# P times V with V stationary, four heads side by side in column tiles

## The chip, the cores and the metric

The kernel runs on one core of one Trainium2 chip. The metric is the device time of one execution, in microseconds (us). Three executions of the kernel before took 3895.41 us in the median, 3886.71 to 3902.54.

## What is computed

Four layers run one after the other over 16 sequences of 256 tokens and 256 channels: layer 0 (two state-space scans, one forward and one backward in time), layer 1 (one scan, with a gather of the tokens by an index and back), layer 2 (attention with 16 heads of 16 channels) and layer 3 (attention with softmax over queries' channels and over keys' tokens). The change touches layer 2 alone. Its core:

```python
q = (xn @ q_w + q_b).reshape(Bx, Tx, H, -1)          # H = 16, 16 channels each
k = (xn @ k_w + k_b).reshape(Bx, Tx, H, -1)
att = jnp.einsum('bnhl,bmhl->bnmh', q, k)
att = att + (1.0 - mask) * -1000000.0
att = jax.nn.softmax(att, axis=2)
v = ((xn @ v_w + v_b) * src_mask[:, :, None]).reshape(Bx, Tx, H, -1)
y = jnp.einsum('bnmh,bmhl->bnhl', att, v).reshape(Bx, Tx, Dx)
```

All numbers are fp32. "P" below is the exponential of the scores, not yet divided by its sum; V carries a 17th column of ones per head, so that the product also holds that sum.

## The kernel before

**Scan units.** The scans are cut into 1,536 units, 96 per batch: three scans (two of layer 0, one of layer 1) of 16 states in two halves of the channels. A unit is a chain over all engines: ACT (line 638) and POOL (line 647) scale the input into `dbut`, PE transposes it into PSUM (`ps_b`, line 563), DVE scans along time (line 667) with the decays that ACT makes (line 628), POOL multiplies the states by C (line 682), which SP has loaded from DRAM six units ahead (line 702, two units in a load), and PE transposes and sums the results in `ps_y` (line 591). The buffers are few (three of `dbut`, `hst` and `g`, four of `decay`), and all engines are in order.

**Ticks and side pieces.** Time in the program is counted in ticks, one per unit. Everything else, the *side pieces*, is written as generators per layer, stage and engine, which stop at each `yield next(at)`. The table `PLACES` gives the tick of every piece, counted from the base of its period; a period is 96 ticks (`PERIOD`). `Between` runs all pieces that are due at a tick: on DVE behind the tick's scan, on SP behind its load of C, on PE between the transposes of unit t+2 (line 563) and the sum of unit t-2 (line 591). In period i the stages belong to different batches: the scans of layer 0 to batch i, layer 1 to i-1 and i-2, the first part of layer 2 (`l2a`) to i-2, its second part (`l2b`), its end (`l2_tail`) and layer 3 to i-3. So the instruction stream is fixed when it is built, and a piece that comes too early holds up its engine.

**The end.** The last scans (32 units of layer 1) start 64 ticks into period 16. `l2b` at ticks 2 to 42 thus runs beside scans for batches 0 to 12, ahead of the last scans for batch 13, and behind all scans for 14 and 15.

**Layer 2.** `l2a` makes `qT` and `kT` (channels of a head on 32 partitions, of which 16 are used and one or two carry the mask and the row maximum; the 16 heads fill four blocks of 128 partitions) and `v2`, computes the scores once for their maxima (line 1263) and transposes the maxima back. `l2b` goes in eight groups of two heads: PE makes the transposed scores of both heads into two PSUM banks (line 1289, `ps_x` banks 0 and 1, keys on partitions, four matmuls of 18 rows by 256), ACT takes their exponential into `pT` (line 1339, 128x1024), and PE multiplies with V (line 1303) into bank 2, P^T stationary in blocks of 128x128, 17 columns of V moving, for 2 heads x 2 blocks of queries x 2 blocks of keys. `pT` exists once, so the exp of a group waits for the product of the last (semaphore `o_full_2`), and the next scores wait for the exp (`p_ready`). The scores of group g stand in the stream ahead of the product of group g-1. After eight heads DVE takes reciprocals of the sums and multiplies (lines 1379 and 1382) into `yv`, and signals `o_taken_2`, for which PE waits before the next eight heads.

`l2_tail` then normalizes, modulates and projects `yv`; `xt_x` is the buffer that it and `l2a` use for turned input. The DMAs that the prediction speaks of are side pieces on SP: the mask of layer 3 (line 1405, which waits for `res_1`, the sum that DVE makes at line 1177), the store of the result (line 1411, which waits for `res_3`) and the loads for layer 0 (lines 889 and 890).

## Time and profile before

| | |
|---|---|
| median of three executions | 3895.41 us (3886.71 to 3902.54) |
| the profiled execution's own time | 3887.06 us |
| its span | 3885.3 us |
| mean granted clock of TensorE | 0.938 of full speed |
| first scan to last scan | 152.5 to 3644.2 us |
| instructions in the span | 66,431 |

One execution was profiled. Its page gives busy times by engine; PE is TensorE's matmuls, PEld its weight loads, which overlap them, DVE is VectorE, ACT ScalarE, POOL GpSimd, SPq the DMA queue of SyncE. A fp32 matmul that is no transpose leaves two records of each kind, a transpose one. The waits give, for each engine that sat idle, what released it. The span is a little shorter than the execution's own time, which is the one that is compared.

### The profile page before, as it was taken

Reading aid. Unit: us, or ns where it says so; the run is one execution under the profiler, and the core shown is the slowest. Engines: PE = TensorE matmul, PEld = TensorE weight load, DVE = VectorE, ACT = ScalarE, POOL = GpSimd, SP = SyncE. Lnnn points to the kernel's source line nnn. Section 1 sums busy time; section 2 is a strip of 40 time slices with the busy share of each in tenths; the row PEclk is TensorE's granted clock in tenths of the full one; section 3 lists DMA queues with packets and bytes.
Section 4 is the critical chain, followed back from the end, with each engine's and each line's share of the span. In section 5 each row is a group of like instructions: output and inputs, shape, how many; then the busy total and the mean of one; then the engine's idle time right before and its main releaser. Section 6 shows DMA issues by size and latency. Waiting matters only on the chain. (4 is left out here: it accounts for less than half of the span.)

```text
span 3885.3 us, 66431 instructions
## 1 busy us (share of the span) xinstructions
PE 3405.1 (88%) x22974; PEld 2923.2 (75%) x22974; DVE 2839.1 (73%) x3589; ACT 2898.8 (75%) x6592; POOL 2859.1 (74%) x3087
## 2 busy tenths in 40 slices
PE   4677788999999998999999998999999899898876
PEld 2466677888888787888878787878878787876655
DVE  0468788787887878787887878787878878773421
ACT  1668788788888888888888788888888788854422
POOL 0478999888887888788888888887888878861400
PEclk9799999999999999999999999999999999997766
DMA  4112222222122212222221212222222212210100
GB/s 163 49 54 80 79 71 79 66 65 78 59 85 59 80 61 79 63 66 78 60 83 59 82 61 80 62 73 69 66 78 61 83 58 73 63 54 18 39 7 3
DMA packets 140814, 257.19 MB, mean 66 GB/s; under 512 B 15905, under 2 KB 33313, under 8 KB 140081
## 3 DMA queue, kind: packets, MB, share of 16 engines
q1 hardware_dynamic: 140482, 252.95, 21.2%
q8 instruction: 186, 3.05, 0.3%
q14 instruction: 146, 1.20, 0.1%
HBM read 233.16 MB, written 5.05 MB: 61 GB/s over the span
## 5 line engine op out<-in xcount | busy, mean ns | idle before, releaser
L682 POOL TENSOR_TENSOR g<-hst,c_bc 128x512 f32<-128x512 f32 x1536 | 1978.3, 1288 | 569.4 <-PE ps_y L591 415.9
L667 DVE TENSOR_TENSOR_SCAN hst<-decay,ps_b 128x512 f32<-128x512 f32 x1536 | 1835.6, 1211 | 509.6 <-PE ps_b L563 244.4
L628 ACT ACTIVATE decay<-delta,acoef 128x256 f32<-128x256 f32 x3072 | 1376.9, 498 | 11.4 <-DVE hst L667 11.0
L563 PE MATMUL ps_b<-ident,dbut 128*128 128x128 f32 x6144 | 964.7, 281 | 267.0 <-DVE hst L667 151.8
L647 POOL TENSOR_TENSOR dbut<-dut,bcm 128x256 f32<-128x256 f32 x1536 | 982.8, 640 | 217.9 <-ACT dut L853 217.9
L563 PEld LDWEIGHTS ps_b<-ident,dbut 128*128 128x128 f32 x6144 | 724.9, 145 | 347.0 <-issue 234.7
L591 PE MATMUL ps_y<-ident,g 128*128 128x128 f32 x6144 | 959.6, 280 | 14.7 <-issue 7.3
L591 PEld LDWEIGHTS ps_y<-ident,g 128*128 128x128 f32 x6144 | 760.5, 145 | 119.3 <-issue 35.2
L638 ACT ACTIVATE dbut<-dut,bcm 128x256 f32<-128x256 f32 x1536 | 767.1, 500 | 53.7 <-PE ps_b L563 50.3
L1303 PEld LDWEIGHTS ps_x<-v,pT 128*128 128x128 f32 x2048 | 276.6, 213 | 31.9 <-issue 28.0
L1303 PE MATMUL ps_x<-v,pT 128*128 128x17 f32 x2048 | 282.6, 277 | 3.2 <-ACT pT L1339 2.3
L1339 ACT ACTIVATE pT<-ps_x 128x1024 f32<-128x1024 f32 x128 | 129.4, 1011 | 123.4 <-PE ps_x L1303 116.1
L1289 PE MATMUL ps_x<-qT,kT 18*128 18x256 f32 x1024 | 164.8, 444 | 20.5 <-ACT pT L1339 19.6
L1364 DVE TENSOR_REDUCE mxt<-ps_x 128x4 f32<-128x1024 f32 x128 | 153.4, 1199 | 12.5 <-PE ps_x L1263 12.5
L1263 PE MATMUL ps_x<-kT,qT 17*128 17x256 f32 x1024 | 149.9, 411 | 6.5 <-DVE mxt L1364 4.2
L617 ACT ACTIVATE xm<-ps_y 128x512 f32<-128x512 f32 x64 | 38.2, 597 | 134.9 <-PE ps_y L591 134.8
L1289 PEld LDWEIGHTS ps_x<-qT,kT 18*128 18x128 f32 x1024 | 98.3, 207 | 54.0 <-ACT pT L1339 27.4
L760 PE MATMUL ps_v<-weights,yg 128*128 128x256 f32 x512 | 133.1, 396 | 3.3 <-DVE yg L1169 1.7
L754 PE MATMUL ps_v<-xt_a,weights 128*128 128x256 f32 x512 | 134.3, 392 | 0.2
L754 PE MATMUL ps_x<-xt_x,weights 128*128 128x256 f32 x512 | 128.2, 390 | 5.2 <-ACT xt_x L1315 5.2
L1263 PEld LDWEIGHTS ps_x<-kT,qT 17*128 17x128 f32 x1024 | 90.3, 190 | 38.8 <-issue 20.4
L860 DVE SCALAR_TENSOR_TENSOR delta<-ps_v,delta 128x512 f32<-128x512 f32 x96 | 64.8, 675 | 62.0 <-ACT delta L841 61.9
(188 smaller groups left out, 4092.1 us busy)
## 6 DMA issues: line engine op xcount, KB each, us to landing
c_bc<-c_rows SPq DMA_DIRECT2D x768, 256.0 KB, 3.2
rows_bc<-mod_rows SPq DMA_DIRECT2D x16, 384.0 KB, 4.4
weights<-in_weights_dram SPq DMA_DIRECT2D x1, 5792.0 KB
ada_w<-in_ada_w_dram SPq DMA_DIRECT2D x1, 5120.0 KB
x<-in_x_dram SPq DMA_DIRECT2D x16, 256.0 KB, 3.8
x0p<-x SPq DMA_DIRECT2D x16, 256.0 KB, 2.5
xr<-x SPq DMA_DIRECT2D x16, 256.0 KB, 3.6
x<-x SPq DMA_DIRECT2D x16, 256.0 KB, 3.6
```

The lines of the kernel that those rows point to most:

```text
L563: last = nc.tensor.matmul(ps_b[:, u % 2, e * T + t * P:e * T + (t + 1) * P], dbut[:, u % NDBU, t, e * P:(e + 1) * P], ident[:, :], is_tran ...
L591: last = nc.tensor.matmul(ps_y[:, t, e * P:(e + 1) * P], g[:, u % NG, e, t * P:(t + 1) * P], ident[:, :], is_transpose=True, start=False, ...
L628: last = nc.scalar.activation(decay[:, u % (DA_AHEAD + 2), e, :], delta[s][:, eb, :], ACT.Exp, scale=acoef[:, s, eb, n:n + 1])
L638: nc.scalar.activation(dbut[:, u % NDBU, 0, :], dut[s][:, 0, hh * HALF * P:(hh + 1) * HALF * P], ACT.Copy, scale=bcm[s][:, 0, n:n + 1]).th ...
L647: nc.gpsimd.tensor_tensor(dbut[:, u % NDBU, 1, :], dut[s][:, 1, hh * HALF * P:(hh + 1) * HALF * P], bcm[s][:, 1, n:n + 1].broadcast_to([P, ...
L667: nc.vector.tensor_tensor_scan(line(hst[:, u % NHST, :, :].rearrange("p e t -> p (e t)")), line(decay[:, u % (DA_AHEAD + 2), :, :].rearran ...
L682: nc.gpsimd.tensor_tensor(g[:, u % NG, :, :], hst[:, u % NHST, :, :], c_bc[:, k % NCB * CHUNK + n % CHUNK, :].unsqueeze(1) .broadcast_to([ ...
L754: last = nc.tensor.matmul(dst, weight[:, k, m0:m0 + m], rhs[:, k, :], start=(k == 0), stop=(k == kb - 1))
L1263: last = nc.tensor.matmul(bank(ps_x, j, TB)[:, q, :], qT[r:r + DH2 + 1, hb, q * P:(q + 1) * P], kT[r:r + DH2 + 1, hb, :], start=True, stop ...
L1289: last = nc.tensor.matmul(bank(ps_x, j, TB)[:, m, :], kT[r:r + DH2 + 2, hb, m * P:(m + 1) * P], qT[r:r + DH2 + 2, hb, :], start=True, stop ...
L1303: last = nc.tensor.matmul(o[:, q, :], pT[:, j, m, q * P:(q + 1) * P], v2[:, m, v, :], start=(m == 0 and q == 0 and v % 8 == 0), stop=(m == ...
L1364: nc.vector.tensor_reduce(by_head[:, 2 * g_:2 * g_ + 2, :, DH2 + 1], ps_x[:, 0:2, :].rearrange("p j (q n) -> p j q n", q=TB), AX.X, ALU.ma ...
```

## The change

- **Groups.** A group of `l2b` is no longer two heads with all keys, but four heads with one block of 128 keys (`half, k, m = g_ // 4, g_ // 2 % 2, g_ % 2`). The scores are still four matmuls of 18 rows by 256, and the exp is still one instruction of 128x1024.
- **The product.** V's 17 columns are stationary, 256 queries of P^T move; four matmuls per group write to partitions 0, 32, 64 and 96 of one half of bank 2, the second block of keys accumulates on the first. The output has a head's channels on partitions.
- **Turned back.** After four groups ACT copies bank 2 to `oT` (the buffer `xt_x`), 128x512, and PE turns it by four transposes into bank 2, in the layout that DVE expects. New semaphores: `ot_sb` and `o_back`. DVE waits for `o_back` instead of `o_full_2`.
- **Heads permuted.** `spread` puts heads in other slots of the query, key and bias layouts, so that the four heads of a group stand in the row tiles that the scores need.
- **Prologue.** One memset of bank 2, since 15 of 32 partitions are never written.
- **Places.** New ticks for side pieces on all engines, most by 0 to 2 ticks, those on SP by more. `l2b` has 19 pieces on PE instead of 25.

```diff
+        oT = xt_x
...
+                    done(nc.vector.memset(ps_x[:, 2, :], 0.0))
...
@@ l2b_tensor
-                    for m in range(TB):
-                        for j in range(2):
-                            h = 2 * g_ + j
-                            r, hb = LANE * (h % HPB), h // HPB
-                            last = nc.tensor.matmul(bank(ps_x, j, TB)[:, m, :], kT[r:r + DH2 + 2, hb, m * P:(m + 1) * P],
-                                                    qT[r:r + DH2 + 2, hb, :], start=True, stop=True)
+                    half, k, m = g_ // 4, g_ // 2 % 2, g_ % 2
+                    for j in range(4):
+                        r, hb = LANE * (2 * k + j % 2), 2 * half + j // 2
+                        last = nc.tensor.matmul(bank(ps_x, j % 2, 2)[:, j // 2, :], kT[r:r + DH2 + 2, hb, m * P:(m + 1) * P],
+                                                qT[r:r + DH2 + 2, hb, :], start=True, stop=True)
...
-                        for q in range(TB):
-                            for m in range(TB):
-                                last = nc.tensor.matmul(o[:, q, :], pT[:, j, m, q * P:(q + 1) * P], v2[:, m, v, :],
-                                                        start=(m == 0 and q == 0 and v % 8 == 0), stop=(m == TB - 1),
-                                                        skip_group_check=True)
+                    half, k, m = (g_ - 1) // 4, (g_ - 1) // 2 % 2, (g_ - 1) % 2
...
+                    for j in range(4):
+                        last = nc.tensor.matmul(bank(ps_x, 2, 2)[LANE * j:LANE * j + DH2 + 1, k, :],
+                                                v2[:, m, 8 * half + 4 * k + j, :], pT[:, j % 2, j // 2, :],
+                                                start=(m == 0 and k == 0), stop=(m == TB - 1), skip_group_check=True)
+                    last.then_inc(S["o_full_2"], 1)
+                if g_ in (H2 // 4, H2 // 2):
+                    yield next(at)
+                    pe.wait_ge(S["ot_sb"], nth("ot_sb", b, g_ // (H2 // 4)))
+                    for k in range(2):
+                        for q in range(TB):
+                            last = nc.tensor.matmul(bank(ps_x, 2, TB)[:, q, k * P:(k + 1) * P], oT[:, k, q * P:(q + 1) * P],
+                                                    ident[:, :], is_transpose=True, start=True, stop=True)
+                    last.then_inc(S["o_back"], 1)
@@ l2b_scalar
+                if g_ % 4 == 3:
+                    yield next(at)
+                    act.wait_ge(S["o_full_2"], nth("o_full_2", b, g_ + 1))
+                    nc.scalar.activation(oT[:, :, :], bank(ps_x, 2, 2), ACT.Copy).then_inc(S["ot_sb"], 1)
@@ l2b_vector
-                dve.wait_ge(S["o_full_2"], nth("o_full_2", b, (half + 1) * H2 // 4))
+                dve.wait_ge(S["o_back"], nth("o_back", b, half + 1))
@@ PLACES, three of the lines
     "l1_in": {
-        "DVE": (2, 7, 13, 14, 15, 15, 16, 19, 19, 20, 22),
+        "DVE": (-4, 7, 12, 14, 14, 15, 15, 18, 18, 19, 21),
     "l2b": {
-        "PE": (2, 4, 11, 12, 14, 14, 15, 19, 19, 21, 25, 26, 26, 29, 29, 29, 31, 32, 34, 36, 36, 38, 40, 40, 42),
+        "PE": (2, 4, 12, 14, 14, 18, 21, 25, 26, 27, 29, 29, 32, 34, 37, 37, 39, 40, 40),
     "l3": {
-        "SP": (9, 18, 95, 171),
+        "SP": (6, 6, 99, 211),
```

How the stream moves, at three places. First PE in a full period, the third group of `l2b` (tick 14) and what stands around it. Before (1289 scores, 1303 product, 591 and 563 the scans' sum and transposes, 754 a projection of layer 0):

```order
L1289 MATMUL ps_x<-qT,kT 128x256 x4
L1303 MATMUL ps_x<-v,pT 128x17 x4
L591 MATMUL ps_y<-ident,g 128x128 x4
L563 MATMUL ps_b<-ident,dbut 128x128 x4
L1303 MATMUL ps_x<-v,pT 128x17 x4
L754 MATMUL ps_v<-xt_b,z1w 128x256 x2
```

Now (1290 scores, 1300 product, 593 and 565 the scans', 756 the projection):

```order
L1290 MATMUL ps_x<-qT,kT 128x256 x4
L1300 MATMUL ps_x<-pT,v 17x256 x4
L756 MATMUL ps_v<-xt_b,z1w 128x256 x2
L593 MATMUL ps_y<-ident,g 128x128 x4
L565 MATMUL ps_b<-ident,dbut 128x128 x4
```

The product is one piece of four matmuls instead of two pieces of four. Second, PE at the end of the first eight heads (ticks 26 to 29), now; 1309 are the transposes back, 781 a projection for a scan:

```order
L1300 MATMUL ps_x<-pT,v 17x256 [waits p_ready]
L1300 MATMUL ps_x<-pT,v 17x256 x3
...
L1309 MATMUL ps_x<-ident,xt_x 128x128 [waits ot_sb]
L1309 MATMUL ps_x<-ident,xt_x 128x128 x3
...
L1290 MATMUL ps_x<-qT,kT 128x256 [waits p_ready]
L1290 MATMUL ps_x<-qT,kT 128x256 x3
L1300 MATMUL ps_x<-pT,v 17x256 [waits o_taken_2,p_ready]
L1300 MATMUL ps_x<-pT,v 17x256 x3
```

Between the product and the transposes stand one unit's sum and transposes, between these and the next scores two more units'. Before, the last product of the eight heads was followed by three units and the scores alone. Third, SP from the store of the result to the loads of C behind layer 3's mask. Before:

```order
L1411 DMA out_dram<-x 128x2x256
L702 DMA c_bc<-c_rows 128x512 x2
L1183 DMA gate<-mod_rows 128x256
L702 DMA c_bc<-c_rows 128x512 x3
L1226 DMA x<-x 128x512
L1405 DMA gate<-in_mask_dram 128x256
L702 DMA c_bc<-c_rows 128x512 x6
```

Now:

```order
L1420 DMA out_dram<-x 128x2x256
L704 DMA c_bc<-c_rows 128x512
L1228 DMA x<-x 128x512
L704 DMA c_bc<-c_rows 128x512
L1414 DMA gate<-in_mask_dram 128x256
L704 DMA c_bc<-c_rows 128x512 x13
```

The mask stands two loads behind the store instead of five, and the load of C behind it is the one placed at tick 8, for units 14 and 15.

## Rows read from the trace of the kernel before

**Rows 1.** The page, busy time (us), share of the span and instructions of the engines
```profile
span 3885.3 us, 66431 instructions
...
PE 3405.1 (88%) x22974; PEld 2923.2 (75%) x22974; DVE 2839.1 (73%) x3589; ACT 2898.8 (75%) x6592; POOL 2859.1 (74%) x3087
```

**Rows 2.** Periods: us, busy of PE, PEld, DVE, ACT, POOL; clock, DMA share, GB/s
```profile
295.30:488.50 193.20, 144.90 (x970) 124.11 (x970) 153.60 (x155) 157.01 (x370) 173.61 (x190) 0.94 0.25 76
488.50:682.80 194.30, 165.73 (x1144) 143.97 (x1145) 159.59 (x181) 159.81 (x378) 177.86 (x193) 0.96 0.24 74
682.80:898.00 215.20, 200.94 (x1429) 176.50 (x1428) 176.06 (x224) 179.75 (x411) 179.50 (x193) 0.98 0.22 69
2617.00:2833.00 216.00, 202.54 (x1418) 177.33 (x1418) 176.14 (x223) 176.78 (x404) 176.92 (x189) 0.96 0.23 67
```

**Rows 3.** Waits in the full periods, us in total, times, longest
```profile
POOL g L682 <- PE ps_y L591: 384.2, 402, 3.6
```

**Rows 4.** Chain of waits, uncovered layer 2: start us, us, engine, tile, line
```profile
3668.92 2.07 PE ps_x L1289 x8
3670.99 3.54 PE ps_x L1303 x16
3674.61 1.03 ACT pT L1339
...
3836.00 1.10 PE ps_x L747 x4
```

**Rows 5.** Timeline of PE in full periods: start us, us, line, op, out<-in, count
```profile
2648.50 0.96 PE L1303 MATMUL ps_x<-v,pT 128*128 128x17 f32 x8
2649.31 0.63 PE L747 MATMUL ps_v<-ident,xn_b 128*128 128x128 f32 x4
...
2652.38 1.03 PE L754 MATMUL ps_v<-xt_b,z1w 128*128 128x256 f32 x4
2653.24 0.60 PE L591 MATMUL ps_y<-ident,g 128*128 128x128 f32 x4
...
2766.54 0.60 PE L591 MATMUL ps_y<-ident,g 128*128 128x128 f32 x4
2766.98 0.60 PE L563 MATMUL ps_b<-ident,dbut 128*128 128x128 f32 x4
2767.51 1.13 PE L1263 MATMUL ps_x<-kT,qT 17*128 17x256 f32 x8
2768.57 0.66 PE L591 MATMUL ps_y<-ident,g 128*128 128x128 f32 x4
```

**Rows 6.** The page's groups: busy, mean ns of one, idle before, of P times V's loads
```profile
L1303 PEld LDWEIGHTS ps_x<-v,pT 128*128 128x128 f32 x2048 | 276.6, 213 | 31.9 <-issue 28.0
```

**Rows 7.** Groups of instructions: an ACT copy from PSUM of this size
```profile
L1114 ACT ACTIVATE xm<-ps_v 128x512 f32<-128x512 f32 x32 | 19.2, 599 | 80.5 <-PE ps_v L754 80.4
```

**Rows 8.** Uncovered windows, line 1303 alone: us, busy PE, PEld; clock, DMA share, GB/s
```profile
3469.50:3583.40 113.90, 23.01 (x128) 22.89 (x128) 0.73 0.06 19
3644.00:3886.00 242.00, 55.55 (x256) 53.91 (x256) 0.65 0.02 8
```

**Rows 9.** Timeline of DVE around the sum of layer 1
```profile
2647.95 0.69 DVE L1177 TENSOR_TENSOR x<-ps_v,xr 128x512 f32<-128x512 f32 x1
...
2650.86 1.22 DVE L667 TENSOR_TENSOR_SCAN hst<-decay,ps_b 128x512 f32<-128x512 f32 x1 [0.86 <-PE ps_b L563]
```

**Rows 10.** DMA issues: count, KB each, median us to landing
```profile
c_bc<-c_rows SPq DMA_DIRECT2D x768, 256.0 KB, 3.2
...
gate<-in_mask_dram SPq DMA_DIRECT2D x16, 128.0 KB, 2.9
```

**Rows 11.** Waits of the whole span, us in total, times, longest
```profile
DVE stats L717 <- DMA rows_bc<-mod_rows: 70.0, 15, 6.4
```

**Rows 12.** Timeline of DVE, the copy ahead of layer 1's norm
```profile
903.22 1.19 DVE L1045 COPY cols<-mod_cols 128x4 f32<-128x4 f32 x1
```

More of the change, by code:

```diff
@@ L160 @@
     "l3": {
-        "PE": (51, 52, 56, 58, 60, 63, 66, 68, 69, 70, 74),
-        "ACT": (49, 51, 61, 65, 66, 69, 70, 78),
-        "DVE": (49, 50, 58, 61, 63, 71, 71, 76, 76, 81, 97),
-        "SP": (9, 18, 95, 171),
+        "PE": (51, 52, 56, 58, 59, 62, 66, 68, 69, 70, 74),
+        "ACT": (50, 52, 60, 65, 66, 69, 70, 80),
+        "DVE": (50, 51, 58, 61, 63, 69, 71, 78, 80, 82, 102),
+        "SP": (6, 6, 99, 211),
     },
     "l3_tail": {
-        "PE": (83, 89, 91, 99),
+        "PE": (84, 90, 92, 103),
         "ACT": (87,),
@@ L1340, in l2b_scalar @@
                                      ps_x[:, 0:2, :].rearrange("p a n -> p (a n)"), ACT.Exp).then_inc(S["p_ready"], 1)
+                if g_ % 4 == 3:
+                    yield next(at)
+                    act.wait_ge(S["o_full_2"], nth("o_full_2", b, g_ + 1))
+                    nc.scalar.activation(oT[:, :, :], bank(ps_x, 2, 2), ACT.Copy).then_inc(S["ot_sb"], 1)
         def l2a_vector(dve, ch, b, at):
@@ L1654, in spread @@
         out = np.zeros((k, H2, 32), m.dtype)
-        out[:, :, :DH2] = m.reshape(k, H2, DH2)
+        slot = [h // 8 * 8 + h // 2 % 2 * 4 + h // 4 % 2 * 2 + h % 2 for h in range(H2)]
+        out[:, slot, :DH2] = m.reshape(k, H2, DH2)
         return out.reshape(k, H2 * 32)
```

76 lines of the change are left out of this document (35 added, 41 removed).

## The prediction

> **What bounds the kernel now.** I read the page's busy shares first [rows 1]: TensorE (PE) is busy 88% of the span, the others 73 to 75%. An average over stages can mislead, so next come the windows of single periods [rows 2]; a period is the 96 scan units of one batch, with its neighbours' side pieces between them. The first has no layer 2, the second the first part of one, the third everything, as all later ones (the fourth row). Going from second to third, PE's busy time rises by 35.2 us and the period by 20.9; DVE, ACT and POOL rise less, and PE ends at 201 of 215. The waits of the full periods [rows 3] say who is late: POOL, which multiplies the states by C, idles 384 us for PE's sums. So PE is the tightest engine there, though not the only one: POOL has 174 to 180 us of work in every period, and periods with less PE work still took 193 to 194 us.
>
> After the scans end, nothing covers layer 2. The chain of waits there [rows 4] is a strict round of scores (2.08), P times V (3.54) and exp (1.03), 6.8 us for each of eight groups; two batches run like that, and a third (3469.5 to 3583.4) nearly so, since the last scans start only after it.
>
> **What P times V costs now.** Per group 16 records of a fp32 matmul (each matmul leaves two), 128 columns of P^T stationary and 17 columns moving. In the timeline [rows 5] eight of them hold PE 0.81 us until the next instruction starts, so a group takes 1.62 and a batch 13.0 us. The page's row of their weight loads [rows 6] shows 277 us busy for 2048: a record is paced by loading 128 columns for 17 of work.
>
> **What it costs after.** A group is four matmuls, eight records: V (17 columns) stationary, 256 columns of P^T moving, each in its own column tile. No row shows column tiles. The nearest is the score product, which has 18 rows, so that neighbours lie in different row tiles. Full-array records of 256 columns take 0.86 us for four (line 754 in [rows 5]), 0.215 each, so eight would need 1.72. Eight records in two row tiles start the next instruction after 1.06 (line 1263 in [rows 5]): four steps of 0.215 and 0.20 of overhead. Entering that mode costs 0.10 more: it starts 0.53 after the previous four transposes began, where 0.44 is usual. So tiles do run side by side, two deep here, for 1.16 us a group.
> - Four column tiles at once, two steps: 1.16 - 0.43 = **0.73 us** a group. I take this, since the row tiles overlapped fully and nothing in the rows separates the two kinds.
> - Two at once: 1.16. One after another, the upper bound: 1.16 + 0.86 = 2.02. The lower bound is the 0.73, since a matmul's two records follow each other.
>
> The Trainium skill, "TensorE: Matmul & The Clock Gate", section "Measured speedup vs the span model", gives three column tiles 2.38 times one. As an estimate by that page, eight records would take 0.72 instead of 0.43 us, and the sum below would be about 23 us higher. No row here can check it.
>
> **The sum in the full periods.** Layer 2's second part runs under scans for 13 batches. Its eight groups cost 8 x 0.73 = 5.8, less 0.4 because in about half of them the product follows the scores directly and the mode change is already paid there. The new transposes back are 2 x 4 at 0.44 us per four (line 591 in [rows 5]): 0.9. Together 6.3 against 13.0: PE saves 6.7 us a batch, 87 in all. How much reaches the period? Rows 2 give 20.9/35.2 = 0.59 between the second and third, and that includes the flat part where POOL decides; at the top it can reach 1. I take 0.75: **-65 us**, ends -51 and -87.
>
> The two copies of PSUM to SBUF on ACT are 128x512 at 0.60 each [rows 7], 1.2 us a batch, beside 177 of 216 us of ACT work. Covered mostly; if ACT were the bound they would be 16 us in 13 batches. I take **+3**. The exp instructions stay eight per batch, and so do DVE's reciprocals and products, which now wait for the transposes instead of the product. PE reaches the next half's first product four groups of scan transposes and a score product after the turn back, so I cost its wait for DVE at nothing. If the wait for ACT's copy ahead of the turn back fails its place, PE stands still and the scans' transposes queue behind it, at most the copy and a little, 1 us a batch.
>
> **The sum without cover.** The product is busy 55.6 us in the last stretch and 23.0 in the one before the last scans [rows 8]. Cold (granted clock 0.65 in this window), the scores' eight records take 2.08 in four steps, so four column tiles take 2.08 - 2 x 0.43 = 1.22. Sixteen groups: 55.6 - 19.5 = 36. The other eight: 23.0 - 8 x 1.0 = 15, of which I count 10, because other pieces share PE there. Added: in each batch the first half's copy (0.60; its transposes lie beside the exp) and the second's copy, transposes (1.10, as line 747 in rows 4) and two hops, 1.9. 2.5 x 3 = 7.5. Net **-38**.
>
> **New places.** Most pieces move by 0 to 2 ticks; their order around the scans stays. Two moves are more.
> - On SP the mask load of layer 3 stands at tick 6 instead of 9, and its wait for the landing too, instead of at 18. It waits for the sum of layer 1, which DVE still makes at tick 12 (it ends at 2648.64 [rows 9]). Then 2.9 us of landing, and only then the load of C for unit 14, 3.2 us [rows 10]: about 2655.1 with both issues. The scan of unit 14 ends at 2652.1 [rows 9]. So POOL gets C 3 us late, and PE, which sums that unit two ticks later, 1.5 us. I take 1.5 x 13 = **+20**, ends 0 and 3 x 13 = 39. The store of the result stands on SP three ticks ahead of DVE's last addition (99 against 102), before it was two; C is loaded six units ahead, so I cost that at nothing.
> - DVE idles 70 us in 15 periods for the rows of layer 0, at tick -2 [rows 11]. The first norm of layer 1 moves from tick 2 to -4, ahead of this wait; its copy alone is 1.19 us [rows 12], with the statistics about 2. It fills idle time: -2 x 15 = -30 at most, 0 if POOL or ACT bind there; I take **-16**.
>
> The whole set can give or take 15 us more by the way stalls fall. The memset in the prologue is under 1 us.
>
> Sum: 3887 (the profiled execution; span 3885.3) - 65 + 3 - 38 + 20 - 16 = **3791 us**, 2.5% less. The profiled time equals the fastest of the three runs; their median is 8 us higher, which I leave within the range.
>
> **Rivals.**
> 1. *Slower: the column tiles do not overlap.* The instruction stream is A, A, B, B, and here all four tiles read the same 128 rows, while line 1263's tiles read different ones. If that is what allows overlap, a group costs 2.02 against 1.62. PE gains no 6.7 but loses 16.2 - 0.4 + 0.9 - 13.0 = 3.7 a batch, 48 x 0.75 = +36; without cover 16 x (3.80 - 3.54) = 4, about 3 for the third batch, and 7.5: +15. With the copies and places: **3945**. It decides from about six steps a group (0.30 + 6 x 0.215 = 1.59) on. Against it: row tiles overlap without loss. The Trainium skill states in the same page, section "The mechanism", that a weight load overlaps matmuls in flight only when the row group differs, which speaks for this rival. In the full-array stream the trace does not bear it out as a bar: records of one row group still follow each other every 0.215, loads hidden.
> 2. *Half overlap: two column tiles at a time.* 8 x 1.16 - 0.4 + 0.9 = 9.8 a batch, 3.2 less: x 13 x 0.75 = -31; without cover 16 x 1.46 + 6 - 7.5 = -22. With the rest: **3841.**
> 3. *The gain is covered.* PE gets shorter, but the periods stay, because POOL (174 to 180 us in each), scans and ACT's pieces set the pace, and places were made for other lengths. Only the uncovered stretches gain, with places and copies at +7: **3856**. For it: periods of 193 us with PE at 145. Against it: POOL's idle time ends on PE.
>
> **Chances.** Forecast 0.50 (own range 3745 to 3825: slope 0.59 to 1, places), rival 2 0.17, rival 3 0.13, rival 1 0.14, other losses by the new places near zero change 0.06. A measurement can tell about 0.5% (19 us) from no change. Faster by more: 0.50 + 0.17 + 0.09 of rival 3 = 0.76. Within: 0.04 of rival 3 and 0.04 = 0.08. Slower: 0.14 + 0.02 = 0.16. The range runs from 3740 to 3885; it leaves out rival 1 and little else.
>
> **What would show it.** Right: the product's records fall from 2048 to 1024, PE busy on them to 5 to 7 us a period, next instruction about 0.63 us after eight of them at full clock; full periods of 209 to 211 us; in the last stretch rounds of about 4.4 us instead of 6.8. Wrong: eight records that hold PE 1.9 us (rival 1) or 1.06 (rival 2), or records near 0.63 with periods still at 215 (rival 3), or a new idle time of PE in front of the transposes back, released by ACT.

## The result and the profile after

The changed kernel took 3852.34 us in the median (3834.64 to 3861.2), the kernel before 3887.25 (3873.91 to 3902.54) over the executions taken beside it: a ratio of 0.9898, 95% interval 0.9879 to 0.9917. It is 1.0% faster. The forecast was 3791 us, 2.5% less: the direction was right, the size was not.

The page of the changed kernel, its first lines as in [rows 1]:

```profile
span 3850.0 us, 64705 instructions
...
PE 3267.6 (85%) x22078; PEld 2693.0 (70%) x22078; DVE 2824.3 (73%) x3590; ACT 2918.2 (76%) x6624; POOL 2854.6 (74%) x3087
```

TensorE has 138 us less work than before, and the span is only 35 us shorter.

**The product itself did what was forecast, and a little more.** The timeline of PE in a full period of the changed kernel (start us, us, engine, line, op, out<-in, count), against [rows 5]. L1300 is the product:

```profile
2669.29 0.60 PE L565 MATMUL ps_b<-ident,dbut 128*128 128x128 f32 x4
2669.82 0.62 PE L1300 MATMUL ps_x<-pT,v 128*17 128x256 f32 x8
2670.38 0.66 PE L593 MATMUL ps_y<-ident,g 128*128 128x128 f32 x4
```

The next instruction starts 0.56 us after the first of the eight records. The group starts 0.53 after the transposes ahead of it, where 0.44 is usual, so it holds PE 0.65 in all, against 0.73 forecast and 1.62 before.

The chain of waits in the uncovered stretch of the changed kernel, two rounds and a way back (start us, us, what); it answers to [rows 4]:

```profile
3772.06 2.08 PE ps_x L1290 x8
3774.14 1.03 PE ps_x L1300 x8
...
3775.25 1.03 ACT pT L1344
...
3776.33 2.08 PE ps_x L1290 x8
3778.41 1.03 PE ps_x L1300 x8
...
3779.46 0.61 ACT xt_x L1349
...
3780.11 1.12 PE ps_x L1309 x4
```

A round takes 4.27 us (3772.06 to 3776.33), 6.8 before, 4.4 forecast. From the last scan to the end the kernel before needs 241.1 us, the changed one 203.5; the stretch ahead of the last scans, in which a third batch lies uncovered, fell from 113.9 to 95.4.

The load of the stationary columns does not stand in the way. The eight loads of the same group (PEld) take 0.13 us together, all four column tiles over the same 128 rows:

```profile
2669.82 0.13 PEld L1300 LDWEIGHTS ps_x<-pT,v 128*17 128x17 f32 x8 [0.17 <-issue]
```

**The full periods gained nothing.** These rows are the windows of the twelve full periods that begin with the third; divided by twelve, the busy times are per period. Layer 2's second part runs in these twelve and in the thirteenth, the "last part" below. First the kernel before, from 682.7 to 3263.8 (us; busy of PE, PEld, DVE, ACT, POOL; clock, DMA share, GB/s):

```profile
682.70:3263.80 2581.10, 2404.70 (x17106) 2109.53 (x17105) 2107.49 (x2673) 2154.66 (x4926) 2150.61 (x2302) 0.98 0.23 70
```

Then the changed kernel:

```profile
690.00:3290.10 2600.10, 2333.80 (x16436) 1967.23 (x16434) 2103.64 (x2673) 2172.43 (x4954) 2144.72 (x2302) 0.98 0.23 69
```

PE works 5.9 us less in a period (200.4 to 194.5), ACT 1.5 more (179.6 to 181.0), and a period went from 215.1 to 216.7 us. The sum of the differences by stretch is that of the spans, within 1 us: start +5, first two periods +2, twelve full periods +19, last part (the thirteenth) -5, ahead of the last scans -18, last scans -1, end -38.

The waits of the changed kernel from 690 to 3400 us (engine, line, waited for, us in total, times, longest); the first answers to [rows 3]:

```profile
POOL g L684 <- PE ps_y L593: 368.9, 350, 4.5
DVE hst L669 <- ACT decay L630: 171.5, 121, 4.2
...
DVE stats L719 <- DMA rows_bc<-mod_rows: 50.6, 11, 6.0
...
PE ps_v L756 <- ACT u L956: 38.6, 24, 1.9
...
POOL g L684 <- DMA c_bc<-c_rows: 31.9, 21, 2.2
```

POOL still waits nearly as long for PE as before (377.2 us in this stretch), although PE has less to do. So a part of PE's lateness is not PE's own work. Where the time went in a period can be read from the starts of the scans, as a mean of the twelve: ticks 40 to 47 took 25.8 us instead of 21.4, ticks 80 to 87 16.5 instead of 14.4, ticks 8 to 23 and 48 to 55 gained 4.4 together.

Two theories stood at first. **A**: the new ticks of the side pieces, which the forecast took at next to nothing, ate the gain. **B**: the full periods are paced by a round over several engines, so PE's time counts only in part.

### The profile page after: what moved, and what is told of

Same layout as the page of the kernel before. It is cut to its first block, busy times and chain, and to the rows that moved or that the text cites. A ratio compares the mean times of both kernels' runs of the same rounds, so it can differ in the third digit from the quotient of the medians.

```text
span 3850.0 us, 64705 instructions
## 1 busy us (share of the span) xinstructions
PE 3267.6 (85%) x22078; PEld 2693.0 (70%) x22078; DVE 2824.3 (73%) x3590; ACT 2918.2 (76%) x6624; POOL 2854.6 (74%) x3087
## 4 chain that ended last, share of the span: by engine, by line
PE 42%; ACT 23%; DVE 12%; issue 8%; POOL 7%; DMA 2%; SPq 0%; DVEq 0%; POOLq 0%; ACTq 0%
PE ps_b L565 8%; PE ps_y L593 8%; ACT decay L630 8%; POOL g L684 5%; DVE hst L669 5%; PE ps_v L756 5%; ACT dbut L640 4%; PE ps_x L762 3%; PE ps_x L756 3%; PE ps_x L1265 3%; POOL dbut L649 2%; PE ps_x L1290 2%; ACT pT L1344 2%; DMA rows_bc<-mod_rows 2%; PE ps_x L765 2%
## 5 line engine op out<-in xcount | busy, mean ns | idle before, releaser
L649 POOL TENSOR_TENSOR dbut<-dut,bcm 128x256 f32<-128x256 f32 x1536 | 972.4, 633 | 201.7 <-ACT dut L855 201.7
L565 PEld LDWEIGHTS ps_b<-ident,dbut 128*128 128x128 f32 x6144 | 715.7, 143 | 367.2 <-issue 227.6
L593 PEld LDWEIGHTS ps_y<-ident,g 128*128 128x128 f32 x6144 | 752.4, 144 | 139.0 <-issue 41.7
L756 PEld LDWEIGHTS ps_v<-xt_a,weights 128*128 128x128 f32 x512 | 91.3, 191 | 25.0 <-DVE yg L1069 9.1
L762 PE MATMUL ps_x<-weights,xt_a 128*128 128x256 f32 x384 | 104.8, 398 | 4.1 <-DVE kmax L1530 1.9
```

The source lines that it names most:

```text
L565: last = nc.tensor.matmul(ps_b[:, u % 2, e * T + t * P:e * T + (t + 1) * P], dbut[:, u % NDBU, t, e * P:(e + 1) * P], ident[:, :], is_tran ...
L593: last = nc.tensor.matmul(ps_y[:, t, e * P:(e + 1) * P], g[:, u % NG, e, t * P:(t + 1) * P], ident[:, :], is_transpose=True, start=False, ...
L649: nc.gpsimd.tensor_tensor(dbut[:, u % NDBU, 1, :], dut[s][:, 1, hh * HALF * P:(hh + 1) * HALF * P], bcm[s][:, 1, n:n + 1].broadcast_to([P, ...
L756: last = nc.tensor.matmul(dst, weight[:, k, m0:m0 + m], rhs[:, k, :], start=(k == 0), stop=(k == kb - 1))
L762: last = nc.tensor.matmul(dst, lhs[:, k, t * P:(t + 1) * P], weight[:, k, :], start=(k == 0), stop=(bias is None and k == kb - 1))
```

## Experiments

Each ratio is to the kernel before, measured beside it. "Period" is the mean of the twelve full periods of the profiled execution; "ahead of last scans" is the stretch from the start of the last unit of period 15 to the start of the next unit, "end" that from the start of the very last unit to the end of the span.

The periods come from one execution each, and executions of one kernel lie up to 42 us apart. Five of the profiled ones lie well above the median of their kernel: those of runs 1, 6 and 12 by 10 to 11 us, of 9 by 7, of 4 by 6. If 10 us lay in the 13 full periods alone, they would be 0.8 us a period. So differences between periods of less than about 1 us are not clear.

| kernel | us, median | ratio, 95% interval | period | ahead of last scans | end |
|---|---|---|---|---|---|
| before | 3887.25 | 1 | 215.1 | 113.9 | 241.1 |
| changed | 3852.34 | 0.9898 [0.9879, 0.9917] | 216.7 | 95.4 | 203.5 |
| mask's ticks as before | 3839.81 | 0.9857 [0.9833, 0.9881] | 216.6 | 98.7 | 199.4 |
| changed, old ticks | 3895.44 | 1.0011 [0.9997, 1.0025] | 217.8 | 109.5 | 208.7 |
| before, new ticks | 3935.53 | 1.0099 [1.0072, 1.0125] | 218.9 | 108.2 | 232.8 |
| before, half the product | 3838.04 | 0.9864 [0.9841, 0.9886] | 212.9 | 110.0 | 217.1 |
| no way back | 3822.54 | 0.9825 [0.9771, 0.9878] | 215.2 | 97.2 | 195.1 |
| one column tile | 3911.26 | 1.0057 [1.0034, 1.0079] | 219.7 | 95.5 | 234.9 |
| half the exp | 3811.54 | 0.9795 [0.9752, 0.9838] | 213.5 | 97.7 | 195.5 |
| late ticks as before | 3831.97 | 0.9854 [0.9809, 0.9900] | 214.2 | 99.2 | 209.5 |
| rows loaded early | 3791.72 | 0.9766 [0.9739, 0.9792] | 212.3 | 94.7 | 204.7 |
| copy on DVE | 3848.44 | 0.9897 [0.9871, 0.9923] | 215.8 | 100.9 | 202.3 |
| sum | 3776.59 | 0.9723 [0.9698, 0.9749] | 210.2 | 101.0 | 202.5 |
| sum, copies later | 3771.28 | 0.9691 [0.9666, 0.9715] | 210.2 | 101.2 | 202.6 |

**1. The mask's ticks as before**, in the changed kernel.

```diff
     "l3": {
-        "SP": (6, 6, 99, 211),
+        "SP": (9, 18, 95, 171),
```

> Measured against the kernel before (3887 us in the median of all its runs, the change 3852). Theory A, the new places eat the gain, of them the mask piece on SP most: POOL's waits for C (31.9 us in 13 full periods after the change) vanish, the full periods fall by 1.5 to 2.5 us each from 216, total 3815 to 3835. Theory B, the full periods are paced by a round over all engines in which the product has no share: POOL idles for PE instead, total 3845 to 3855.

The period did not move (216.6), though its profile is the slowest of six executions, 10 us above their median. The median, 3839.81, lies between the two forecasts. And this was no clean test of the mask. The DMA queue's own waits, first of the changed kernel, from 690 to 3400 us (L1414 is the mask's load, L1420 the store of the result):

```profile
SPq L1414 <- DVE x L1179: 138.4, 13, 14.2
SPq L1420 <- DVE x L1557: 84.2, 12, 7.3
```

Then of this one:

```profile
SPq L1420 <- DVE x L1557: 185.9, 12, 17.0
...
SPq L1414 <- DVE x L1179: 88.0, 13, 9.7
```

The old ticks bring the store forward to 95 while DVE's last addition stays at 102, and SP stands up to 17.0 us there. POOL then waited 68.3 us in 22 times for C instead of 31.9 in 21. One wait on SP was exchanged for another, and the period stayed: what the mask's tick is worth alone stays unresolved. The medians differ by 12 us, and the two intervals touch.

**2. The new product with the ticks of before, 3. the old product with the new ticks.** In both, `l2b` keeps the ticks of its own product; all other rows of `PLACES` are exchanged. Two of the rows for kernel 2 (for kernel 3 the signs turn round):

```diff
     "prep1": {
-        "PE": (46, 49, 66, 70, 77, 89, 94, 101),
+        "PE": (46, 49, 66, 70, 77, 89, 94, 98),
...
     "l1_in": {
-        "DVE": (-4, 7, 12, 14, 14, 15, 15, 18, 18, 19, 21),
+        "DVE": (2, 7, 13, 14, 15, 15, 16, 19, 19, 20, 22),
...
```

> The new product with the places of the kernel before, except those of the second part of layer 2. Theory A (places eat the gain): full periods of 209 to 211 us, total 3775 to 3800. Theory B (the product's time was covered): full periods stay at 214 to 217, total 3840 to 3865.

> The old product with the new places, except those of the second part of layer 2. Theory A (the new places cost what the product gives): full periods of 220 to 222 us, total 3950 to 3980. Theory B: full periods of 214 to 217, total 3875 to 3900.

Kernel 2 came out above both forecasts (3895 us, 217.8), kernel 3 between them (3936 us, 218.9). The new ticks alone cost the old product 1.0%: 3.8 us a period. The parts far from the product show it best: ticks 80 to 87 took 16.5 us with the new ticks and 14.4 with the old, whichever product was in. The old ticks cost the new product 1.1%, but only 1.1 us of it in each of the twelve periods; 7 us lie in the thirteenth, 14 ahead of the last scans and 5 at the end. Within a period they lose at one place what they gain at others: ticks 24 to 31 took 27.5 us instead of 20.4, ticks 40 to 47 21.3 instead of 25.8 and ticks 80 to 87 14.4 instead of 16.5. The timeline of kernel 2 there, ACT and PE (idle time before in brackets):

```profile
1843.26 0.60 ACT L1349 ACTIVATE xt_x<-ps_x 128x512 f32<-128x512 f32 x1 [5.27 <-PE ps_x L1300]
...
1845.07 1.28 ACT L987 ACT_TABLE_LOAD   x1
...
1847.44 1.28 ACT L989 ACT_TABLE_LOAD   x1
1848.74 1.02 ACT L1344 ACTIVATE pT<-ps_x 128x1024 f32<-128x1024 f32 x1
1849.78 1.28 ACT L1123 ACT_TABLE_LOAD   x1
...
1853.15 1.28 ACT L1128 ACT_TABLE_LOAD   x1
...
1853.23 1.09 PE L593 MATMUL ps_y<-ident,g 128*128 128x128 f32 x4 [7.67 <-issue]
```

ACT waits for the product before its copy, and then four function tables and the work between them, due at neighbouring ticks, run in one piece of 9.4 us, in which no decay and no `dbut` for the scans comes. So product and ticks belong together, theory A holds as far as that, and what one half of the change is worth depends on the other:

| us a period | old ticks | new ticks |
|---|---|---|
| old product | 215.1 | 218.9 |
| new product | 217.8 | 216.7 |

With the old ticks the new product costs 2.7 us a period, with the new ones it saves 2.2.

**4. Half of the product left out**, in the kernel before.

```diff
-                            for m in range(TB):
+                            for m in range(1):
...
-                                                        start=(m == 0 and q == 0 and v % 8 == 0), stop=(m == TB - 1),
+                                                        start=(m == 0 and q == 0 and v % 8 == 0), stop=(m == 0),
```

> The kernel before with half of the product left out: only the first block of keys is multiplied, so its results are not the reference's. PE does 6.5 us less in every full period, with no new copy, turn or place; uncovered, a round of the last stretch falls from 6.8 to about 5.0 us. Theory A (less PE time shortens the periods by 0.75 of it): 13 x 4.9 = 64 and about 35 without cover, total 3785 to 3795. Theory B (covered): the full periods stay within 1.5 us of 215, total 3845 to 3860.

PE's work fell from 200.4 to 194.1 us a period, the period by 2.2: 0.35 us for each us of PE. The forecast had 0.75. The total, 3838, lies below B's 3845 and far above A's 3795, so this speaks for B. The clock went down beside it: in ticks 40 to 51 the granted clock was 0.90 to 0.95 in all twelve periods, and these ticks took 32.8 us in the mean. In the kernel before it was 1.00 in seven periods (31.1 us) and 0.95 in five (32.8).

**5. No way back**, in the changed kernel: `act` and `pe` lose the copy and the four transposes, DVE waits for `o_full_2`. Here and in run 6 the memset in the prologue also writes 1.0 instead of 0.0.

```diff
-                    pe.wait_ge(S["ot_sb"], nth("ot_sb", b, g_ // (H2 // 4)))
-                    for k in range(2):
-                        for q in range(TB):
-                            last = nc.tensor.matmul(bank(ps_x, 2, TB)[:, q, k * P:(k + 1) * P], oT[:, k, q * P:(q + 1) * P],
-                                                    ident[:, :], is_transpose=True, start=True, stop=True)
-                    last.then_inc(S["o_back"], 1)
...
-                    act.wait_ge(S["o_full_2"], nth("o_full_2", b, g_ + 1))
-                    nc.scalar.activation(oT[:, :, :], bank(ps_x, 2, 2), ACT.Copy).then_inc(S["ot_sb"], 1)
...
-                dve.wait_ge(S["o_back"], nth("o_back", b, half + 1))
+                dve.wait_ge(S["o_full_2"], nth("o_full_2", b, (half + 1) * H2 // 4))
```

> The changed kernel without the way back: ACT's copy of 128x512 (two a batch) and TensorE's four transposes (two a batch) are left out, DVE waits for the product itself; so the output of layer 2 is not what the reference computes. It prices the way back. Theory A (the new ticks took the gain of the full periods; the way back is covered there): full periods 216.7 stay within 0.5 us, and only the uncovered batches gain, 2.5 times about 3 us (copy, transposes and hops, twice a batch): 8 us less, 3844. Theory B (the full periods are paced by a round over several engines in which ACT and PE alternate, ACT 0.9 busy at ticks 24 to 48): copy and transposes (2.4 us a batch) count by half, full periods 215.5, 3828 in all.

1.5 us a period, somewhat over B's 1.2, where A had none, and 8.4 us at the end. The way back is not covered. The run takes 1.0 us of ACT and 1.2 of PE off a period, and does not tell which of the two counts.

**6. One column tile**, in the changed kernel.

```diff
-                        last = nc.tensor.matmul(bank(ps_x, 2, 2)[LANE * j:LANE * j + DH2 + 1, k, :],
+                        last = nc.tensor.matmul(bank(ps_x, 2, 2)[0:DH2 + 1, k, :],
```

> The changed kernel with the outputs of all four heads of a group on partitions 0 to 16, one column tile, so that three of four are overwritten and the output of layer 2 is not the reference's; instructions, sizes and waits are the same. It shows what column tiles are worth. If the tile makes the overlap, eight records take eight steps of 0.215 instead of two: 1.9 us a group instead of 0.66, 9.9 us of PE a batch more; uncovered, with the clock at half, some 2.4 us a group, 16 groups, and 8 x 1.5 for the third batch: 50 us. If records with 17 stationary columns overlap whatever their tile, nothing changes. In full periods: Theory B (slope of 0.35, as half of the product left out showed) gives 3.5 us a period, total 3852 + 13 x 3.5 + 50 = 3948. A slope of 0.75, as the prediction had it, gives 7.4 us a period and 3998. Theory A says nothing on the slope.

The timeline of PE:

```profile
2697.10 1.90 PE L1300 MATMUL ps_x<-pT,v 128*17 128x256 f32 x8
2698.93 0.66 PE L593 MATMUL ps_y<-ident,g 128*128 128x128 f32 x4
```

1.83 us until the next starts, eight steps of 0.215 and 0.11, against 0.56 with four tiles, two steps and 0.13. The edit changes the column tile, with the output's partitions that go with it, and nothing else on PE: the tile makes the overlap. PE's work rose from 194.5 to 202.2 us a period, the period by 3.0: 0.39 for each us of PE, from the other side (0.29, if the 10 us by which this profile lies above its median were all in the periods). The uncovered stretches lost 31 us, not the 50 expected; that is half of the 37 us by which the total stayed under its expectation.

**7. Half of the exp**, in the changed kernel.

```diff
-                                                v2[:, m, 8 * half + 4 * k + j, :], pT[:, j % 2, j // 2, :],
+                                                v2[:, m, 8 * half + 4 * k + j, :], pT[:, 0, j // 2, :],
...
-                nc.scalar.activation(pT[:, :, :, :].rearrange("p a t n -> p (a t n)"),
-                                     ps_x[:, 0:2, :].rearrange("p a n -> p (a n)"), ACT.Exp).then_inc(S["p_ready"], 1)
+                nc.scalar.activation(pT[:, 0:1, :, :].rearrange("p a t n -> p (a t n)"),
+                                     ps_x[:, 0:1, :].rearrange("p a n -> p (a n)"), ACT.Exp).then_inc(S["p_ready"], 1)
```

> The changed kernel with the exp of layer 2's second part over 512 of 1024 columns (both heads of a pair read the same half, so the output is not the reference's): ACT works about 0.42 us less a group, 3.4 us a batch, TensorE and DVE the same. Theory B, with ACT as a bound at ticks 24 to 48: full periods shorter by 1.5 to 3.4 us, 214 us, total 3852 - 13 x 2.5 - 2.5 x 8 x 0.42 = 3811. If ACT is no bound there, only the uncovered batches gain: 8 us, 3844.

The windows of its twelve full periods:

```profile
697.20:3259.10 2561.90, 2325.29 (x16437) 1961.24 (x16436) 2098.44 (x2672) 2131.12 (x4953) 2143.05 (x2302) 0.98 0.23 70
```

ACT's work fell by 3.4 us a period (181.0 to 177.6), the period by 3.2: 0.92 for each us of ACT. Period and total (3811.54) are those of theory B. The exp is also a link of the round of scores, exp and product, so the run does not separate ACT's load from the length of that round. But run 5 and run 10, which take the copies off ACT, fit a slope near 1. So the engine that the page shows at 76% is worth more than twice as much per microsecond, beside the product, as the one at 85%. It is short in one part of the period. These are the windows of ticks 24 to 47 in the eighth period, kernel before:

```profile
1809.80:1867.80 58.00, 56.18 (x404) 50.01 (x404) 39.81 (x54) 53.49 (x108) 46.14 (x50) 0.97 0.20 60
```

and the changed kernel:

```profile
1821.40:1885.60 64.20, 56.49 (x382) 45.66 (x380) 39.98 (x54) 56.99 (x117) 47.52 (x52) 0.92 0.18 54
```

ACT is busy 92% of it before and 89% now, with six of the eight table loads of a period (1.28 us each) in these ticks; PE went from 97% to 88%. And PE has 22 records less but no less busy time, at a granted clock of 0.92 instead of 0.97. This is one period, and one of the longer; the mean of these ticks is 58.2 us before and 62.3 in the changed kernel.

**8. The late ticks as before**, in the changed kernel: the rows of `PLACES` for `prep0`, `prep1`, `l0_post`, `l2a`, `l2_tail`, `l3` and `l3_tail` on PE, ACT and DVE, and `l3` on SP. For example:

```diff
     "l3": {
-        "DVE": (50, 51, 58, 61, 63, 69, 71, 78, 80, 82, 102),
-        "SP": (6, 6, 99, 211),
+        "DVE": (49, 50, 58, 61, 63, 71, 71, 76, 76, 81, 97),
+        "SP": (9, 18, 95, 171),
```

> The changed kernel with the ticks of before for all pieces that stand behind tick 42 of a period: the last parts of layers 0, 2 and 3 (prep0, prep1, l0_post, l2a, l2_tail, l3, l3_tail) on PE, ACT and DVE, and layer 3's mask on SP; those of layer 2's product, of layer 1 and of layer 2's scan input stay new. Theory A: the scans of ticks 44 to 51 and 80 to 87 get the old times back (2 us each), full periods 212.5 instead of 216.6, total 3852 - 52 = 3800, with the mask's 12 us perhaps 3790. Theory B (a round over engines): the time moves elsewhere in the period, full periods within 1 us of 216.6, total 3840.

The period fell by 2.45 us, ticks 40 to 47 from 25.8 to 22.2, ticks 80 to 87 from 16.5 to 15.4; the waits for C fell from 31.9 to 10.6 us. Twelve periods give 29 us, but the end and the stretch ahead of the last scans took 10 us more, so the total gained 20 and not 52, between the two forecasts; its interval overlaps that of the changed kernel. So the shorter period is shown, a faster kernel is not. What ticks 40 to 51 lost is to be seen in the timeline of the changed kernel:

```profile
1862.48 0.66 PE L1309 MATMUL ps_x<-ident,xt_x 128*128 128x128 f32 x4 [0.65 <-ACT xt_x L1349]
1864.48 1.60 PE L756 MATMUL ps_v<-xt_b,z2w 128*128 128x256 f32 x4 [1.34 <-ACT u L956]
1865.87 1.06 PE L593 MATMUL ps_y<-ident,g 128*128 128x128 f32 x4
...
1874.64 1.58 PE L762 MATMUL ps_x<-weights,xt_x 128*128 128x256 f32 x4 [1.88 <-ACT xt_x L1211]
```

PE waits three times for ACT, the first time for the new copy, which stands on ACT ahead of `u`. Behind the second wait four records take 1.39 us until the next instruction, 0.86 at full clock. The windows of ticks 40 to 51, the changed kernel:

```profile
1858.60:1894.70 36.10, 28.44 (x179) 23.71 (x177) 27.57 (x46) 29.36 (x69) 25.07 (x28) 0.91 0.16 47
```

and kernel 8:

```profile
1854.60:1885.80 31.20, 25.06 (x175) 20.80 (x173) 28.25 (x47) 28.35 (x66) 23.48 (x25) 1.00 0.17 55
```

The kernel before has 31.2 us and a clock of 1.00 there too. With 0.91, TensorE ran part of this stretch at 1.2 GHz instead of 2.4. But this period shows the difference at its largest. The seventh period of the changed kernel has the same instructions at a clock of 1.00:

```profile
1642.70:1675.50 32.80, 25.30 (x179) 21.18 (x177) 28.89 (x47) 29.43 (x69) 25.19 (x28) 1.00 0.17 53
```

Over the twelve periods, ticks 40 to 51 took:

| kernel | clock 1.00 | 0.95 | 0.91 | mean |
|---|---|---|---|---|
| before | 7 times, 31.1 us | 5 times, 32.8 | | 31.8 |
| changed | 4 times, 32.8 us | once, 34.8 | 7 times, 36.1 | 34.9 |
| late ticks as before | 2 times, 31.2 us | 10 times, 32.9 | | 32.6 |

So of the 2.3 us that run 8 gains here, 1.6 are there at full clock too and belong to the ticks; the rest goes with the clock, which differs from period to period in one and the same kernel. That the pauses made the clock fall is read from their order in the timeline and was not tried by itself.

**9. Rows loaded early**, in the changed kernel.

```diff
     "l0_in": {
-        "SP": (-4, -4),
+        "SP": (-8, -4),
```

> The changed kernel with the load of layer 0's rows and input on SP at tick -8 instead of -4; the wait for its landing stays at -4. In the traces of both kernels the load is issued only about 1.5 us before DVE comes to it and lands 4.8 us later, whatever stands ahead of it on DVE; so moving the norm of layer 1 ahead of that wait could not shorten it, since the load moves with the ticks. Theory A (the wait is one of issue time): DVE's 50 us for these rows in the full periods falls under 10, and as DVE's scan is the next link there, tick -2 gets 3 to 4 us shorter: full periods 213.5, total 3852 - 42 = 3810. Theory B (ACT and POOL have 160 to 180 us of work and are behind by then anyway): DVE's idle time goes over to decays or g, full periods 216, total 3845.

The change moved a norm ahead of DVE's wait for these rows and the forecast counted 16 us for it. The changed kernel's DVE:

```profile
1761.23 0.74 DVE L719 BATCH_NORM_STATS2 stats<-x 128x6 f32<-128x256 f32 x2
...
1768.63 0.75 DVE L719 BATCH_NORM_STATS2 stats<-x 128x6 f32<-128x256 f32 x2 [4.17 <-DMA rows_bc<-mod_rows]
```

and its DMA queue:

```profile
1763.58 0.39 SPq L891 DMA_DIRECT2D x<-in_x_dram  x1
1764.02 0.46 SPq L892 DMA_DIRECT2D rows_bc<-mod_rows  x1
```

The norm of 1761.23 now stands ahead, and the wait is as long as before, 68.4 us in 15 over the span against 70.0 [rows 11]: the load is issued by SP at its tick, which moves with the scans, and lands 4.6 us later in any case. With the load four ticks earlier (issued at 1740.39, DVE comes to it at 1749.0 without idle time), 9.5 us in 2 are left:

```profile
  DVE stats L719: 9.5, 2
```

The scan behind tick -2 came 2.0 us after the one before it instead of 6.7 (means of twelve). The period fell by 4.3, and so did the eight ticks around it (88 to 95, 15.6 us instead of 19.9): nothing of it was lost elsewhere. Theory A holds, and its forecast for this run, 3810, was still too careful: 3791.72. One number in one table is worth more (1.3% against the changed kernel) than the whole change (1.0%).

**10. The copy on DVE**, in the changed kernel.

```diff
-                    nc.scalar.activation(oT[:, :, :], bank(ps_x, 2, 2), ACT.Copy).then_inc(S["ot_sb"], 1)
...
+                dve.wait_ge(S["o_full_2"], nth("o_full_2", b, (half + 1) * H2 // 4))
+                nc.vector.tensor_copy(oT[:, :, :], bank(ps_x, 2, 2)).then_inc(S["ot_sb"], 1)
     "l2b": {
-        "ACT": (3, 13, 16, 25, 26, 27, 30, 36, 39, 40),
-        "DVE": (29, 42),
+        "ACT": (3, 13, 16, 25, 27, 30, 36, 39),
+        "DVE": (26, 29, 39, 42),
```

> The changed kernel with the copy of the product's output made by DVE instead of ACT, at ticks 26 and 39; same result. Half of the exp left out on ACT had shortened a full period by nearly all that it saved (3.2 of 3.4 us), the product's time on PE counted by a third. Theory B: the copy costs its 0.57 us on ACT in full, so two of them off it give 1.1 us a period, less 0.3 for DVE: full periods 215.9, total 3842. Theory C (whatever waits for the product waits in the scans' chain, on DVE more so than on ACT): DVE stands at each copy until the product is done, full periods 1 us or more longer, total 3865.

The period fell by 0.9 to B's 215.8, though a step this small is not clear of the spread; the stretch ahead of the last scans took 5.5 us more, and the whole is no different from the changed kernel within the measurement. DVE stands in a new wait:

```profile
DVE xt_x L1382 <- PE ps_x L1300: 67.8, 25, 3.2
```

**11. The sum** of 8, 9 and 10, with the changed kernel's late ticks kept for periods 16 to 18 by a second table (`SPECIAL`).

```diff
 SPECIAL = {
+    i: {
+        "prep0": {
+            "PE": (45, 48, 49, 53, 60, 69, 70, 71),
...
+    } for i in range(16, 19)
 }
```

> All that seemed to help in one kernel, same result: the product of the change, the copy on DVE, layer 0's load four ticks earlier, the ticks of before for the pieces behind tick 42 and the mask of layer 3, but the new ticks for all of these in the uncovered stretch at the end (periods 16 to 18). Expected by adding: full periods 216.7 - 2.4 (late ticks) - 0.8 (copy) - 3.1 (rows) = 210.4, end 200 us: 3852 - 13 x 6.3 - 3 = 3767. If the parts share one bound, they do not add: 3800.

210.2 us a period. The expectation's 210.4 counts 3.1 us for the rows, where run 9 measured 4.3; with the three periods as measured the sum would be 216.7 - 2.45 - 4.3 - 0.9 = 209.0. So 6.5 of 7.7 us came: the parts share no bound, or little of one. The ratio is the one that the three ratios give by adding, 0.972. The stretch ahead of the last scans took 101.0 us, as with the copy on DVE alone (100.9), and the total is 10 us above the 3767 expected. By the ratios it is 1.8% under the changed kernel and 2.8% under the kernel before.

**12. The copies one tick later**, in the sum.

```diff
-        "PE": (2, 4, 12, 14, 14, 18, 21, 25, 26, 27, 29, 29, 32, 34, 37, 37, 39, 40, 40),
-        "DVE": (26, 29, 39, 42),
+        "PE": (2, 4, 12, 14, 14, 18, 21, 25, 26, 28, 29, 30, 32, 34, 37, 37, 39, 41, 41),
+        "DVE": (27, 30, 40, 42),
```

> The sum of the last series with DVE's copies one tick later (27 and 40), and the transposes back, the normalization and the product behind it one tick later too. In the sum's profile DVE stood 70 us in 26 waits for the product ahead of its copy, and the scans of ticks 26 and 39 took 5.0 and 4.0 us instead of 1.7 and 1.1, though 27, 28 and 40 gave part back. Theory C (a place that is late for the product is cheaper than a DVE that waits for it): full periods 209.0 to 209.7 instead of 210.2, total 3765. Theory A': the wait only moves to PE in front of the transposes back: 210.2, total 3777.

DVE's wait fell from 70.0 us in 26 to half:

```profile
DVE xt_x L1421 <- PE ps_x L1339: 33.5, 26, 2.0
```

and the period stayed at 210.2: ticks 32 to 39 gained 2.9 us, ticks 40 to 47 lost 3.0. That is A', in the period. But the profile is the slowest of six executions, 11 us above their median, and the median of 3771.28 us lies halfway between C's 3765 and the 3777 of A', so C is not ruled out. The median is the lowest of all, and its interval overlaps that of the sum.

## Why the prediction was right or wrong

The uncovered stretches were forecast at -38 us, and gained 56. The full periods were forecast at -58 (-65 + 3 + 20 - 16), and the thirteen with layer 2's second part lost 14. Kernel 3 splits these 14: the new ticks alone cost +49 in the thirteen periods, where the forecast had +4, and the product with its way back then gave -35, where the forecast had -62. Two steps failed, the price of the new ticks and the slope.

**Right: the price of the product.** Four column tiles overlap in full. The forecast's 0.73 us a group, which it also named as the lower bound, was 0.65: the fixed part was 0.13 and 0.09, not the 0.20 and 0.10 of the row tiles. Rival 1 (2.02) and rival 2 (1.16) fell, and run 6 shows that the tile makes the difference. The Trainium skill, "TensorE: Matmul & The Clock Gate", section "Measured speedup vs the span model", has 2.38 for three column tiles. Here four tiles give 1.83/0.56 = 3.3; the steps went from eight to two, a factor of 4 without the fixed 0.1 us. The Trainium skill, the same page, section "The mechanism", lets a weight load overlap only where the row group differs. Here the trace does not agree: all tiles read the same 128 rows, their eight loads took 0.13 us together and their matmuls ran side by side, so the rule is no bar for this form.

**Right: the stretches without cover.** Forecast -38 net. Between kernel 3 and the changed one, which share the late ticks, they differ by 12.8 and 29.3: 42 us. A cold product group measured 1.03 us, not 1.22. By the new ticks these stretches gained another 14 (kernel before to kernel 3), which the forecast had not counted.

**Wrong: the slope of 0.75.** "I take 0.75: -65 us" was the largest term. The slope was taken from two periods that differ in the work of all engines at once (20.9/35.2), and it was then raised on the thought that at the top PE decides. Changing PE alone gives 0.35 (run 4) and 0.39 (run 6), ACT alone gives 0.92 (run 7). With these the product's part of a period is an estimated -5.9 x 0.37 = -2.2 us, not -5.0, and kernel 3 against the changed one has -2.2 too. Part of the low slope may be the clock: its means of ticks 24 to 47 are 0.97 before, 0.95 in the changed kernel and 1.00 with one column tile, where PE has most to do. POOL's 384 us of waiting for PE [rows 3] names only the last link; PE itself waits for others, in the changed kernel for ACT ahead of the transposes back and of `u`.

**Wrong: "covered mostly", +3 for ACT's copies.** A share of 82% over a period said nothing of ticks 24 to 47. ACT's work rose by 1.5 us a period; at 0.92 that is an estimated +1.4 us, 18 in all. Run 5 gives 1.5 us a period for copies and transposes together, run 10 gives 0.9 for moving the copies to DVE. So the bound that the prediction named and did not take, 16, was nearer than the 3.

**Wrong: moves of 0 to 2 ticks at nothing.** The new ticks cost the old product 3.8 us a period (kernel 3); restoring the ones behind tick 42 in the changed kernel gives 2.45 (run 8), 32 in 13. The prediction put such losses at 15 us at most for the whole set. It also took the moves for smaller than they are: "Two moves are more" leaves out, among others, a piece of `l0_in` on PE that went from tick 38 to 30 and two on SP that went from 2 and 9 to -27. Which of the moves costs the time was not tried. The terms -2.2, +1.4 and +2.45 add up to +1.7, and the measured difference is +1.6. That is in part luck: the three come from different kernels, and with the old ticks the same product costs +2.7.

**Wrong: -16 for the norm.** The wait was not one for DVE to fill; see run 9.

**+20 for the mask: the mechanism is there, its price is not known.** SP's wait for the sum grew (95 to 138 us in the stretch from 690 to 3400 us). C came late for unit 14, as the prediction said, in each of the thirteen periods there, by 0.8 to 2.2 us, 1.3 in the mean, where it had 3; the other eight of the 21 waits are for unit 84. SP also stood 154.9 us in 12 waits for another sum of DVE (line 1032), 8.4 before. No run isolates what either costs.

So the picture of rival 3 is what came: the full periods stayed, the uncovered stretches gained. It had 0.13 and named 3856. Its reason was only half right, and its number in part luck. It said that POOL, the scans and ACT's pieces set the pace and that the places were made for other lengths. The runs bear out ACT's pieces and the places. But PE's gain was not covered: it counted by a third, new ticks took it back, and the uncovered stretches gained 18 us more than it said.

## What to carry to other kernels

In a kernel of many engines in lockstep, the price of an engine's microsecond is a slope to be measured at the place of the change: take some work off one engine alone, then off the next. Here the busiest engine had 0.35 and 0.39, and one at 76% had 0.92. An edit that moves work from the first to the second has to be priced at both rates. New places for everything else are a change of their own, to be measured with the old work in them. And look at every wait for a DMA for when the transfer is issued: here it was issued a moment before its use, reordering the waiting engine did not shorten the wait, and issuing it earlier did at once.

## What the hardware showed beside that

- Four column tiles over the same 128 rows: eight fp32 records of 256 columns in 0.56 us, the same in one tile 1.83. One load of 17 stationary columns takes 96 ns, eight in four tiles 0.13 us together, hidden under a step of 0.215.
- Going over to a tiled form costs PE about 0.1 us (0.53 instead of 0.44 from the transposes ahead to the group), and the way out about as much (0.56 for two steps of 0.215).
- ACT's function table loads take 1.28 us; there are 8 a period in every kernel here, 10.3 us, and the cost of their place can be far higher than their own: where four of them and the work between stood together (kernel 2), PE stood still for 7.7 us.
- The granted clock of one stretch jumps between a few values from period to period: ticks 40 to 51 of the changed kernel took 32.8 us at 1.00 in four periods and 36.1 at 0.91 in seven, the same instructions; four records of 256 columns took 1.39 us there instead of 0.86.
- Less work on TensorE went with a lower clock: with half the product left out of the kernel before (run 4), ticks 40 to 51 had 0.94 in the mean instead of 0.98, and 32.8 us instead of 31.8.
